# Eight pad writes moved from SyncE to GpSimd, and one DMA transpose issued ahead of a row load

## The reference

```python
x = x + ssm(layernorm(x))            # s, B, scan h = h A^T + u over 4096 steps, C, D, times a gate
def ffn(x, gate_w, expert_w):        # on layernorm(x)
    scores = einsum('bsh,eh->bse', x, gate_w)
    onehot = one_hot(argmax(scores, -1), 8)
    expert_out = einsum('bsh,efh->bsef', x, expert_w)
    return x + einsum('bsef,bse->bsf', expert_out, onehot)
x = x + ffn(layernorm(x))
```

## Time and profile before

| | |
|---|---|
| median of 3 runs | 925.98 us (925.22 to 927.23) |
| the profiled execution, its own time | 928.0 us |
| its span (first to last instruction) | 926.3 us |
| TensorE matmuls busy | 904.1 us, 98% |
| VectorE, ScalarE, GpSimd busy | 704.2, 597.2, 389.8 us |
| TensorE clock granted, mean | 0.996 |

### The profile page before, as it was taken

The page is one execution under the profiler, slowest core; times in us unless marked ns, Lnnn a source line. Parts: engine busy times, 40 slices in busy tenths (PEclk is TensorE's granted clock), DMA queues, the critical chain, the costliest instruction groups (busy, mean ns, idle before and its releaser), DMA issues.

```text
span 926.3 us, 15829 instructions
## 1 busy us (share of the span) xinstructions
PE 904.1 (98%) x4565; PEld 739.5 (80%) x4566; DVE 704.2 (76%) x1725; ACT 597.2 (64%) x826; POOL 389.8 (42%) x492
## 2 busy tenths in 40 slices
PE   8999999999999999999999999999999999999995
PEld 7777888888888888888888888888868887888884
DVE  6778979788888979788888979788787465555552
ACT  5568676857767675867767685857534345666661
POOL 1032536181634536181634527181623453333432
PEclk9999999999999999999999999999999999999998
DMA  8435384746657474748557485846789868999881
GB/s 311 131 91 140 89 206 114 205 108 171 151 140 187 89 198 120 204 111 171 153 137 186 90 199 118 206 113 178 254 275 413 336 234 243 224 218 219 192 187 39
DMA packets 203593, 165.55 MB, mean 179 GB/s; under 512 B 128245, under 2 KB 161781, under 8 KB 202496
## 3 DMA queue, kind: packets, MB, share of 16 engines
q1 hardware_dynamic: 192576, 130.89, 55.6%
q0 software_dynamic: 10800, 33.70, 10.7%
q10 hardware_dynamic: 144, 0.07, 0.0%
HBM read 81.63 MB, written 54.68 MB: 147 GB/s over the span
## 4 chain that ended last, share of the span: by engine, by line
PE 88%; DVE 3%; issue 2%; SPq 1%; ACT 1%; DMA 1%; POOL 0%; ACTq 0%; DVEq 0%; POOLq 0%
PE y L1662 19%; PE y L1382 7%; PE y L1383 7%; PE y L1384 7%; PE gates L1382 7%; PE gates L1384 6%; PE gates L1383 6%; PE scan L1527 3%; PE turned L1568 3%; PE gates L1568 3%; PE scan L1382 2%; PE scan L1383 2%; PE scan L1384 2%; PE turned L1650 2%; PE scores L1484 2%
## 5 line engine op out<-in xcount | busy, mean ns | idle before, releaser
L1662 PE MATMUL y<-experts,x1T_hi 128*128 x568 | 180.7, 399 | 2.6 <-issue 2.5
L578 POOL TENSOR_SCALAR ln_var_eps<-ln_mean_var 128x4 f32<-128x4 f32 x16 | 3.6, 224 | 302.3 <-DVE ln_mean_var L1017 302.2
L1662 PEld LDWEIGHTS y<-experts,x1T_hi 128*128 128x128 f32 x568 | 103.4, 188 | 24.1 <-issue 4.2
L623 POOL DMA_INDIRECT out<-gate,ids x71 | 72.0, 1015 | 111.1 <-DVE gate L1347 68.2
L1662 PE MATMUL y<-experts,x1T_lo 128*128 x284 | 111.4, 392 | 0.0
L1347 DVE TENSOR_TENSOR gate<-y,raw_weights 128x512 f32<-128x512 f32 x71 | 49.1, 691 | 75.6 <-PE y L1662 50.4
L1382 PE MATMUL gates<-GwT_hi,xT_hi 128*128 128x512 f32 x256 | 104.6, 409 | 0.0
L1382 PE MATMUL y<-DwT_hi,xT_hi 128*128 128x512 f32 x256 | 101.8, 398 | 0.5 <-DVE gateT L939 0.5
L731 ACT ACTIVATE joined<-flipped 128x1024 uint16<-128x1024 uint16 x60 | 82.3, 1371 | 29.7 <-DVE xT_lo L1167 21.1
L1383 PE MATMUL y<-DwT_lo,xT_hi 128*128 128x512 f32 x256 | 100.3, 392 | 0.0
L1384 PE MATMUL y<-DwT_hi,xT_lo 128*128 128x512 f32 x256 | 100.3, 392 | 0.0
(11 more groups left out here) (276 smaller groups left out, 2340.9 us busy)
## 6 DMA issues: line engine op xcount, KB each, us to landing
raw_weights<-routed_rows SPq DMA_DIRECT2D x71, 258.0 KB
x_in<-L_attn_x SPq DMA_DIRECT2D x32, 512.0 KB, 5.0
x_rows<-L_attn_x SPq DMA_DIRECT2D x32, 512.0 KB, 4.9
turned_experts<-raw_weights SPq DMA_DIRECT2D x32, 512.0 KB, 5.3
experts<-turned_experts SPq DMA_DIRECT2D x8, 2048.0 KB
raw_weights<-L_ffn_expert_w SPq DMA_DIRECT2D x32, 256.0 KB, 3.1
routed_rows<-padrow SPq DMA_DIRECT2D x9, 258.0 KB
out<-gate,ids POOLq DMA_INDIRECT x71
```

Source lines behind the costliest of these rows:

```text
L623: nc.gpsimd.indirect_dma_start(out=out_rows, out_offset=bass.IndirectOffsetOnAxis(ap=ids[r][:, 0:1], axis=0), in_=res[r], in_offset=None, ...
L1662: ins = nc.tensor.matmul(Y[m % 2][:], x2T[a][:, k, m % 2 * P:(m % 2 + 1) * P], flat[:, bass.ds(first + (w * KD + k) * D, D)], start=(k == ...
```

## The change

The eight pad writes leave SyncE and become eight indirect DMAs of GpSimd, two behind each of the slots 20 to 23. Their 128 destinations come from a tile `pad_at` of 128x8 integers, the list ends plus the partition's number, which VectorE makes with one addition in the place of the copy into `end_rows`; the partition numbers `p_iota` are made at the start of the kernel by one more iota of GpSimd. The waits for the constants go from 4 to 5. On SyncE the row loads of slots 24 to 27 follow each other directly, the wait for `ends_ready` is gone, and `flip_odd(1)`, the DMA transpose of slot 25, stands ahead of the row load of slot 28 instead of behind it. `flip_odd(3)`, of slot 27, stays behind the row load of slot 30. Before slot 48 SyncE now waits for `pads_placed` too.

```diff
-        end_rows = kb("list_end_rows", [1, E], i32)
+        pad_at = kb("pad_rows", [P, E], i32)
+        p_iota = kb("partition_iota", [P, E])
...
-            sp.wait_ge(S_["ends_ready"], 1)
             for m in range(M):
+                if m == 4:
+                    flip_odd(1, LOOSE)
                 load_slot(LOOSE * M + m, m)
-                if m < 4:
-                    for e in (2 * m, 2 * m + 1):
-                        end = sp.value_load(end_rows[0:1, e:e + 1], min_val=0, max_val=DUMMY - P)
-                        sp.dma_start(routed[bass.ds(end, P), :], padrow[:]).then_inc(S_["pad_sent"], 16)
-                elif m % 2 == 0:
-                    flip_odd(m - 3, LOOSE)
+                if m == 6:
+                    flip_odd(3, LOOSE)
...
-            sp.wait_ge(S_["pad_sent"], 16 * (E + 1))
+            sp.wait_ge(S_["pad_sent"], 16)
+            sp.wait_ge(S_["pads_placed"], 16 * E)
...
-                                        (slot_iota[:], [[1, TABLE]], 0)):
+                                        (slot_iota[:], [[1, TABLE]], 0), (p_iota[:], [[0, E]], 1)):
...
+            def pads(first, n):
+                pool.wait_ge(S_["ends_ready"], 1)
+                for e in range(first, first + n):
+                    nc.gpsimd.indirect_dma_start(
+                        out=routed, out_offset=bass.IndirectOffsetOnAxis(ap=pad_at[:, e:e + 1], axis=0),
+                        in_=padrow[:], in_offset=None).then_inc(S_["pads_placed"], 16)
...
                 elif 17 <= s < 17 + NT:
                     scatter(LASTB, 1, [s - 17])
+                if s >= LOOSE * M - E // 2:
+                    pads(2 * (s - LOOSE * M) + E, 2)
...
-                    nc.vector.tensor_copy(end_rows[:], run[0:1, :]).then_inc(S_["ends_ready"], 1)
+                    nc.vector.tensor_tensor(pad_at[:], run[:], p_iota[:], ALU.add).then_inc(S_["ends_ready"], 1)
```

More of the change, by code:

```diff
@@ L191, in preln_ssm_moe_kernel @@
                      "scoresT_psum scoresT_ready scores_psum scores_ready top_ready sig_warm hit_ready cand_ready best_ready onehot_ready "
-                     "rank_psum pos_ready picked_ready run_ready dest_ready ids_ready ends_ready pad_sent "
+                     "rank_psum pos_ready picked_ready run_ready dest_ready ids_ready ends_ready pad_sent pads_placed "
                      "experts_in table_step slot_iota_made expert_table need_table row_table "
@@ L1278, in _ @@
             dve.wait_ge(S_["cols_loaded"], 16 * (KH + 2))
-            dve.wait_ge(S_["consts2_made"], 4)
+            dve.wait_ge(S_["consts2_made"], 5)
             for b in range(NBLK):
@@ L1424, in _ @@
             prep(0)
-            pe.wait_ge(S_["consts2_made"], 4)
+            pe.wait_ge(S_["consts2_made"], 5)
             def dense(dst, i, w, ks, closed):
```

## The result

| | before | after |
|---|---|---|
| median | 926.03 us (925.22 to 927.23, 6 runs) | 931.68 us (930.64 to 932.42, 6 runs) |
| the profiled execution, own time | 928.0 | 931.68 |
| its span | 926.3 | 929.9 |

The ratio is 1.0059, with a 95% interval of 1.0046 to 1.0072: the change costs about 5.6 us. The forecast was 923.6, within 922.6 to 926.3.

A forecast was written before the change was run, and what follows sets the result against it. TensorE, busy 98% of the span, was taken to bound the kernel, so only its idle time could pay. Saving 1.91 + 0.5 = 2.4 us from the median of 925.98 gave 923.6 us, range 922.6 to 926.3.

The forecast's parts named there:

- the price of GpSimd's eight indirect DMAs: GpSimd behind slots 20 to 23: 1.26 us each, row numbers late but with 1.5 us to spare, so cost nothing.
- The transpose: SyncE, slot 25: issued about 766.65 instead of 769.82, landing at 771.6, so ScalarE's join no longer waits for it.
- Its worth, 1.91 us: TensorE at 776: the late turn and the late product behind it, 1.22 + 0.69 us, both saved by the earlier transpose.
- the 2.4 us: Whole forecast saving: 1.91 from the stall at 776 plus 0.5 near 760.
- The 0.5 near 760: TensorE ahead of slot 20: a slow register load while pads fill the DMA engines loses 0.56 us; 0.5 saved.
- A: Rival, slot 25's transpose: pads in flight delay its landing, so the join still waits; about 925.2 us, chance 0.20.
- B: Rival: GpSimd falls behind, late row numbers stall TensorE near 788; slower, 928.0 at 1.8 us per DMA, chance 0.08.
- C: Rival, TensorE at 776: stall only changes hands, SyncE, ScalarE or VectorE late for a hidden reason; 925.3 us, chance 0.12.

The follow-up runs named there:

- c2: The kernel before with two 128x384 additions on GpSimd behind each of slots 20 to 23, no further DMA: 925.04 us, 1.0002.
- b3: The kernel before, SyncE's pads kept, with eight more GpSimd indirect DMAs of 128 rows, 16 bytes each, behind slots 20 to 23: 931.36 us, 1.0057.
- c3: The kernel before with ScalarE writing the pads behind slots 17 to 23 and slot 25's transpose ahead of slot 28's row load: 925.08 us, 0.9992.
- a2: The kernel before with only slot 25's transpose moved ahead of slot 28's row load; SyncE still writes the pads: 926.03 us, 0.9996.
- c1: The kernel before with SyncE's pads spread, four behind row loads 24 to 27, then the transposes, four among the next eight loads: 925.49 us, 1.0003.
- b1: The changed kernel with GpSimd's pads spread, one behind each of slots 21 to 28: 927.5 us, 1.0013.
- d2: The kernel before, unchanged, profiled a second time: 925.75 us, 1.0004.
- a3: The changed kernel, with SyncE waiting for all eight pads to land before issuing slot 25's transpose: 941.1 us, 1.0157.
- b4: The kernel before, SyncE's pads kept, with eight more plain GpSimd DMAs of 2064 bytes a row, without an index list: 932.99 us, 1.0076.
- a4: The changed kernel with GpSimd's pads spread, one behind each of slots 17 to 22 and two behind slot 23: 933.36 us, 1.0073.

## Why the prediction was wrong

**The step that failed** is the price of GpSimd's eight indirect DMAs, put at nothing: "Cost nothing, but this is the thinnest cover". Their duration was right: 0.96 us, one of them 1.18, and 0.30 before each. Wrong was the list of who could suffer, only what is queued behind them on GpSimd. The runs show the loss on TensorE's signals to ScalarE and VectorE, engines that have nothing to do with GpSimd's queue: c2 keeps GpSimd busy and loses nothing, b3 adds eight indirect DMAs of 16 bytes a row and loses 5.3 us (0.57% of 926). Priced by after's rows the term of nothing is 6.4 us: 0.79 + 0.70 + 3.52 behind late signals and 1.40 for the clock behind them.

**The transpose** was right in mechanism: it was issued at 765.52, and ScalarE joins without a wait. In the changed kernel that proves little, since the join comes 5 us late anyway (777.24); c3 shows it undisturbed, the join at 771.14 right behind the normalising at 770.44.

**Its worth, 1.91 us,** was mis-sized. It was read from one execution that was 2.0 us above the median and carried over "as it is". That stall was 1.9, 1.4 and 0.1 us in three profiles with SyncE's order of before. Three versions that take the stall away without GpSimd's DMAs (a2, c1, c3) change the time by 0.3 parts in a thousand upwards to 0.8 downwards, and the intervals of a2, c1 and c3 leave 1.7 us at most. So even without the loss little of the 2.4 us would have been seen, and 923.6 was not to be expected; no run has the changed kernel without late signals, so how much it would be stays open.

**The 0.5 near 760** was right, in size and cause. The product follows the turn by 0.46 there after against 0.92, 0.46 less, and the register load ahead of it (last line) took 302 ns where the earlier trace rows has 568. In b1 too, with no pad before 765, it took 303; in a2, c1, c2, c3 and d2, where pads are still written near 758, it took 687 to 912.

```profile
759.56 0.60 PE L1659 MATMUL scores<-ident,raw_weights 128*128 128x128 f32 x4
760.02 0.73 PE L1671 MATMUL y<-experts,x1T_hi 128*128 x2
...
L1665 PEldq TENSOR_LOAD <-slot_need x1: 302/302/302, 758.3 to 758.3; - x1
```

**Rivals.** A wanted the join to wait for the DMA; it doesn't, and a3 rules out that the meeting of pads and transposes makes the loss (b4 shows that A's mechanism exists). B had the sign, "slower", but another place, price and condition: it was to start at an indirect DMA above 1.40 us and to stall near 788. Of the ten up to 774 one passed that, with 1.18 + 0.31 = 1.49, and the idle time is at 774 to 777. (The slots' order in B is the kernel's: a row load waits for the slot eight before it, 24 for 32, not for the seventh, as it stands under "A slot".) The row numbers of slot 24 were copied at 781.47 instead of 778.7, because GpSimd's queue waited 3.22 us for the held-back result of slot 22; no later turn waits for them. C's picture, an idle TensorE at 776 with another releaser, is what the trace shows in form, but by a cause that nothing in the profile of before, as I read it, had suggested.

**It could have been seen.** In the first stage of the kernel before, four scatters follow each other (619.76, 621.17, 622.43, 623.70, each 0.96 to 1.10 us), and three of TensorE's signals there come at 625.60 to 625.68, 1.25, 1.17 and 0.52 late (at 334.4, behind four like scatters, up to 1.59); ScalarE starts line 680 only at 625.62. TensorE has other work there and never stands, so neither waits nor chain point to it.

## What to carry to other kernels

Before putting DMAs on GpSimd behind DMAs that it already has, look at how long its row becomes without a pause, not only at whether GpSimd keeps up: here two a slot with a 0.7 us pause behind them were free, and four or more in a row delayed an engine that doesn't touch them. Where ScalarE or VectorE wait "remote", or the chain has an unknown queue, compare the signal's time with the end of the work that should send it. And a stall read from one execution above the median can be more than its removal brings: profile the kernel a second time before pricing it.

## What the runs showed of the hardware

- A row of GpSimd's indirect DMAs of 128 rows, 1.27 us apart without a pause, delays TensorE's semaphore updates, and the latest come 1 to 2 us after its end: ten DMAs, up to 6.4 us late; seven, up to 4.7 (b3); six, up to 3.5 (a4); four, up to 1.6 (first stage of the kernel before). The bytes don't matter (16 or 2064 a row). No update of ScalarE, VectorE or GpSimd was found late from 700 to 810 us of any profile; the DMAs' own completions bunch too (after: 32 of the pads' within 775.72 to 777.17), and some records of them are missing, so they may be held as well. What holds them no run here settles; nor how long a pause has to be to free them: with 0.9 us behind every second DMA (b1, to 771) nothing was late, with 0.35 behind every third (a4) it was.
- The same eight pads cost 5.6 us from GpSimd (931.68) and nothing that can be measured from SyncE spread out (925.49) or from ScalarE (925.08). The Trainium skill (DMA: Bandwidth & Descriptors, section "Issuing engines are not separate DMA queues") says that initiating DMAs on several engines at once saves only the sequencer's time to initiate them. These runs show a further cost on GpSimd's side.
- After 3.35 us without a matmul (774.15 to 777.50, in the changed kernel) the granted clock went to 0.50, the 1.2 GHz level, for 3.4 us once TensorE worked again, 1.4 us of the loss.
